# A new order for the steps of all eight chunks on TensorE, ScalarE, GpSimd and VectorE, with two waits moved into their step

## The reference

```python
# part A: projection, causal convolution of 4 taps, then running sums
z = conv(x @ in_proj_w) + conv_b                  # values, gate, scores
p_w = exp(clip(score_scale * s_raw, -20, 20)) * time_weight
phi = x5 * theta;  poly = w[0] + w[1] * x5 - w[2] * x5**2
num_re, num_im, den = cumsum([p_w*poly*cos(phi), p_w*poly*sin(phi), p_w], axis=1)
y = (re * rs * norm @ W_re + im * rs * norm @ W_im) * silu(gate) @ out_proj_w
# part B: autocorrelation with the context
corr = irfft(rfft(Q) * conj(rfft(K)), axis=2).mean(-1)
w, idx = top_k(corr, 5);  out = sum_k softmax(w)_k * roll(V, idx_k) @ Wo
# part C: 8 experts, twice (forward and inverse branch), with a router
prod = (Q_side @ V) * cumsum(K_side @ W, axis=1)
weights = softmax(gelu(Q_side @ router_w1.T) @ router_w2.T + expert_bias)
out = einsum(prod * weights, U) / n_valid
```

## Time and profile before

| | |
|---|---|
| median of 3 runs | 940.35 us (939.72 to 940.51) |
| profiled execution, first to last instruction | 936.6 us |
| around the span, against the median | 3.75 us |
| TensorE busy | 847.8 us, 91% |
| VectorE busy | 760.2 us, 81% |
| ScalarE busy | 528.3 us, 56% |
| GpSimd busy | 106.3 us, 11% |

### The profile page before, as it was taken

One profiled execution on the slowest core, in us unless ns is written; L12 is line 12 of the kernel. 1 busy time (PEld: TensorE's weight loads), 2 busy tenths in 40 slices (PEclk: granted clock), 3 DMA queues, 4 the chain that ended last, 5 costly groups with the idle time before them and its releaser, 6 DMA issues.

```text
span 936.6 us, 11711 instructions
## 1 busy us (share of the span) xinstructions
PE 847.8 (91%) x4072; PEld 505.2 (54%) x4072; DVE 760.2 (81%) x1290; ACT 528.3 (56%) x853; POOL 106.3 (11%) x206
## 2 busy tenths in 40 slices
PE   3499848999999999999999999999999998997896
PEld 1145535564756465646565465646556565656344
DVE  6898898899999997899979898999789994473232
ACT  3674871876478554875377456765476644312311
POOL 2020011200310012001200031001210031001001
PEclk9689988999999999999999999999999999999898
DMA  9860242101611052204310071004410250000000
GB/s 298 166 133 4 67 91 45 48 1 19 128 35 45 9 111 62 68 10 77 71 40 7 1 135 45 1 1 90 114 46 0 40 119 0 1 1 23 0 1 22
DMA packets 38768, 50.96 MB, mean 54 GB/s; under 512 B 15236, under 2 KB 30903, under 8 KB 38711
## 3 DMA queue, kind: packets, MB, share of 16 engines
q0 software_dynamic: 7008, 25.21, 14.1%
q1 hardware_dynamic: 31558, 24.62, 9.2%
q10 hardware_dynamic: 144, 0.39, 0.1%
HBM read 20.81 MB, written 4.19 MB: 27 GB/s over the span
## 4 chain that ended last, share of the span: by engine, by line
PE 72%; DVE 15%; ACT 7%; issue 3%; POOL 1%; DMA 0%; ACTq 0%; DVEq 0%; POOLq 0%
PE ps L791 12%; PE ps L771 11%; PE ps L780 11%; PE ps L654 6%; PE ps L593 6%; PE ps L736 4%; PE ps L576 3%; PE ps L624 3%; DVE zc L2484 3%; DVE sc L2563 3%; PE ps L453 2%; PE ps L713 2%; PE ps L638 2%; PE ps L703 2%; PE ps L788 1%
## 5 line engine op out<-in xcount | busy, mean ns | idle before, releaser
L2563 DVE TENSOR_TENSOR_SCAN sc<-mask,sc 128x1024 f32<-128x1024 bf16 x64 | 146.2, 2285 | 0.4
L780 PE MATMUL ps<-x2t,mv 128*128 128x512 f32 x256 | 123.5, 605 | 0.1
L771 PE MATMUL ps<-cum,mw 128*128 128x512 f32 x256 | 123.0, 603 | 0.0
L791 PE MATMUL ps<-up,prod 128*128 128x256 f32 x512 | 115.6, 381 | 0.1
L791 PEld LDWEIGHTS ps<-up,prod 128*128 128x128 f32 x512 | 94.8, 190 | 19.3 <-issue 5.1
L2311 POOL DMA_DIRECT2D acc<-sq x48 | 42.0, 874 | 536.0 <-ACT sq L1535 523.9
L1629 ACT ACTIVATE cs<-ps 128x512 f32<-128x512 f32 x64 | 38.0, 593 | 113.8 <-PE ps L771 113.8
L2555 DVE TENSOR_TENSOR sc<-sc,g 128x1024 f32<-128x1024 f32 x64 | 77.3, 1207 | 7.2 <-ACT sc L1519 7.2
L771 PEld LDWEIGHTS ps<-cum,mw 128*128 128x128 f32 x256 | 48.2, 192 | 62.1 <-issue 60.0
L593 PE MATMUL ps<-sc,wy 64*64 64x512 f32 x512 | 66.6, 644 | 15.2 <-DVE zc L2484 8.2
L1535 ACT ACTIVATE sq<-sc 128x1024 f32<-128x1024 f32 x48 | 50.5, 1053 | 46.3 <-DVE sc L2563 33.7
(11 more groups left out here) (248 smaller groups left out, 1446.7 us busy)
## 6 DMA issues: line engine op xcount, KB each, us to landing
acc<-sq POOLq DMA_DIRECT2D x48, 512.0 KB, 4.6
xt<-in_x_t_dram SPq DMA_DIRECT2D x8, 512.0 KB, 4.4
xs_a<-in_x_dram SPq DMA_DIRECT2D x8, 512.0 KB, 3.8
cin<-in_ctx_dram SPq DMA_DIRECT2D x8, 512.0 KB, 4.8
out_dram<-prod SPq DMA_DIRECT2D x16, 256.0 KB, 2.1
win<-in_in_proj_dram SPq DMA_DIRECT2D x1, 544.0 KB, 6.1
prod<-in_L_ffn_V_fwd_dram SPq DMA_DIRECT2D x2, 256.0 KB
prod<-in_L_ffn_W_fwd_dram SPq DMA_DIRECT2D x2, 256.0 KB
```

The costliest lines, as they stand in the source:

```text
L771: last = mm(o, mw[:, t, br, c:c + P], cum[:, t, :], start=(t == 0), stop=(t == 1))
L780: last = mm(o, mv[:, t, br, c:c + P], x2t[:, t, :], start=(t == 0), stop=(t == 1))
L791: return mm(o[:, (q % 2) * D:(q % 2 + 1) * D], prod[:, j, q * P:(q + 1) * P], up[:, j, :], start=start, stop=False)
L2563: V.tensor_tensor_scan(flat, mask[:, 0:2 * T], flat, 0.0, ALU.mult, ALU.add)\
```

## The change

No instruction is added or taken away. In the four lists the same calls stand in another order: of the 569 places of TensorE 377 hold another call, of ScalarE's 587 480, of VectorE's 577 387, of GpSimd's 81 8 (four pairs of neighbouring additions swapped). SyncE's list of transfers is as it was. Two waits that stood in TensorE's list between `fold(25)` and `b_transform(0, "cf", 0)` are now at the top of that step. Places of the lists that the steps below speak of, from TensorE, ScalarE and VectorE in turn; most of the rest is of the same kind:

```diff
@@ -630,6 +630,9 @@
             def b_transform(i, name, t):
 
                 src = ch if name == "cf" else xh
+                if is_first(i) and name == "cf" and t == 0:
+                    pe.wait_ge(folded, len(FOLD))
+                    pe.wait_ge(ready, 2)
                 pe.wait_ge(*VEC_B.at(i, "fold", 1 if name == "cf" else 3))
                 o = free_b(i, name, t)
                 for b in range(SEQ):
@@ -815,11 +818,11 @@
...
             a_scores(0)
             a_project(0, 0)
             a_project(0, 1)
-            a_spread(0, 0)
-            fold(0)
-            a_spread(0, 1)
             a_project(0, 2)
             a_project(0, 3)
+            fold(0)
+            a_spread(0, 0)
+            a_spread(0, 1)
             a_sums(0, 0)
             a_sums(0, 1)
...
             fold(8)
+            a_sums(0, 2)
+            a_sums(0, 3)
             fold(9)
             fold(10)
-            a_sums(0, 2)
-            a_sums(0, 3)
+            fold(11)
             a_squares(0)
-            fold(11)
             fold(12)
+            fold(13)
+            fold(14)
             a_factor(0, 0)
-            fold(13)
             a_factor(0, 1)
             a_scores(1)
             a_out(0, 0)
             a_project(1, 0)
             a_out(0, 1)
-            fold(14)
+            fold(15)
...
             b_back(6)
             c_out(5, 0)
             c_out(5, 1)
-            a_sums(7, 2)
             b_out(6, 0)
             b_out(6, 1)
+            a_squares(7)
+            a_sums(7, 2)
             a_sums(7, 3)
-            a_squares(7)
+            a_factor(7, 0)
             b_transform(7, "cf", 0)
+            a_factor(7, 1)
             b_transform(7, "cf", 1)
-            a_factor(7, 0)
             c_transpose(6, 0)
             c_transpose(6, 1)
-            a_factor(7, 1)
+            a_out(7, 0)
             c_hidden(6, 0)
-            a_out(7, 0)
             c_hidden(6, 1)
             a_out(7, 1)
             c_hidden(6, 2)
+            c_running(6, 0)
             c_hidden(6, 3)
-            c_logits(6)
-            c_running(6, 0)
-            c_turn(6)
...
             c_hidden(7, 3)
+            c_running(7, 0)
             c_logits(7)
-            c_running(7, 0)
+            c_running(7, 1)
             c_turn(7)
             c_own(7, 0)
+            c_own(7, 1)
             c_weights(7)
+            c_running(7, 2)
             c_spread(7, 0)
-            c_running(7, 1)
             c_spread(7, 1)
-            c_last(7, 0)
-            c_own(7, 1)
-            c_running(7, 2)
+            c_running(7, 3)
             c_spread(7, 2)
             c_own(7, 2)
-            c_running(7, 3)
             c_spread(7, 3)
+            c_spread(7, 4)
+            c_running(7, 4)
+            c_running(7, 5)
             c_own(7, 3)
-            c_running(7, 4)
-            c_spread(7, 4)
             c_own(7, 4)
-            c_running(7, 5)
+            c_own(7, 5)
             c_spread(7, 5)
-            c_own(7, 5)
             c_running(7, 6)
+            c_running(7, 7)
             c_spread(7, 6)
+            c_spread(7, 7)
+            c_last(7, 0)
+            c_last(7, 1)
             c_own(7, 6)
-            c_running(7, 7)
-            c_spread(7, 7)
-            c_last(7, 1)
+            c_own(7, 7)
             c_last(7, 2)
             c_last(7, 3)
             c_last(7, 4)
             c_last(7, 5)
-            c_own(7, 7)
...
             a_scores(0)
-            a_exp(0)
             a_project(0, 0)
             a_project(0, 1)
             a_turns(0, 0)
-            a_turns(0, 1)
+            a_project(0, 2)
+            a_project(0, 3)
+            a_exp(0)
             a_linear(0, 0)
             a_linear(0, 1)
+            fold(0)
+            a_turns(0, 1)
             a_angles(0, 0)
+            a_angles(0, 1)
             a_turns(0, 2)
-            fold(0)
-            a_angles(0, 1)
             a_turns(0, 3)
-            a_project(0, 2)
-            a_project(0, 3)
-            a_gate(0, 0)
-            a_gate(0, 1)
+            a_angles(0, 2)
+            a_angles(0, 3)
             a_guard(0)
-            a_angles(0, 2)
...
             fold(1)
+            a_gate(0, 0)
             fold(2)
...
             a_conv(0, 0)
+            a_conv(0, 1)
+            a_conv(0, 2)
+            a_fraction(0, 0)
             a_split(0)
+            a_conv(0, 3)
+            a_poly(0, 0)
+            a_fraction(0, 1)
+            a_poly(0, 1)
             a_den(0)
-            a_conv(0, 1)
-            a_fraction(0, 0)
-            a_fraction(0, 1)
-            a_poly(0, 0)
-            a_poly(0, 1)
             a_moments(0, 0)
             a_fraction(0, 2)
-            a_scan(0, 0)
             a_moments(0, 1)
             a_fraction(0, 3)
+            a_scan(0, 0)
             a_scan(0, 1)
-            a_conv(0, 2)
-            a_conv(0, 3)
             a_moments(0, 2)
+            a_moments(0, 3)
...
+            a_moments(7, 7)
             a_scan(7, 6)
-            a_moments(7, 7)
+            a_scan(7, 7)
             b_back(6)
-            a_scan(7, 7)
             c_residual(5, 0)
             c_residual(5, 1)
+            b_fold(7, "cf")
             b_residual(6, 0)
+            a_weight(7)
             b_residual(6, 1)
-            a_weight(7)
-            b_fold(7, "cf")
             a_factor(7)
```

More of the change, by code:

```diff
@@ L846, in _ @@
             a_out(0, 1)
-            fold(14)
+            fold(15)
             a_project(1, 1)
-            fold(15)
             fold(16)
             fold(17)
+            a_spread(1, 0)
+            a_project(1, 2)
             fold(18)
@@ L965, in _ @@
             a_project(3, 1)
-            a_spread(3, 0)
+            a_project(3, 2)
             c_hidden(1, 1)
@@ L1245, in _ @@
-            a_project(7, 2)
-            a_project(7, 3)
-            c_weights(5)
             b_spectrum(6, "qa")
             b_spectrum(6, "qb")
+            c_turn(5)
+            c_own(5, 0)
+            c_running(5, 1)
             b_spectrum(6, "ka")
-            c_spread(5, 0)
             b_spectrum(6, "kb")
             b_spectrum(6, "va")
+            c_weights(5)
             b_spectrum(6, "vb")
-            c_running(5, 1)
+            c_spread(5, 0)
+            c_running(5, 2)
             c_spread(5, 1)
@@ L1271, in _ @@
+            c_own(5, 5)
             b_wt(6)
-            c_own(5, 5)
-            c_running(5, 6)
             c_spread(5, 6)
+            b_wf(6)
             c_own(5, 6)
-            b_wf(6)
-            a_sums(7, 1)
             c_running(5, 7)
@@ L1280, in _ @@
             c_own(5, 7)
+            a_sums(7, 1)
             b_back(6)
@@ L1703, in _ @@
             fold(10)
+            a_gate(0, 1)
+            fold(11)
             a_norm(0)
+            fold(12)
+            fold(13)
+            fold(14)
             a_scores(1)
@@ L1775, in _ @@
             a_project(2, 0)
+            a_exp(2)
+            c_hidden(0, 0)
+            a_linear(2, 0)
+            a_turns(2, 0)
             b_transform(1, "cf", 0)
             b_transform(1, "cf", 1)
-            a_project(2, 1)
-            c_hidden(0, 0)
+            c_hidden(0, 1)
             a_layer(1)
-            c_hidden(0, 1)
             c_hidden(0, 2)
             c_hidden(0, 3)
-            a_turns(2, 0)
+            a_project(2, 1)
+            a_angles(2, 0)
+            c_logits(0)
@@ L1796, in _ @@
-            a_project(2, 2)
-            b_spectrum(1, "qa")
             b_spectrum(1, "qb")
-            b_spectrum(1, "ka")
-            a_project(2, 3)
+            c_weights(0)
+            a_angles(2, 2)
             b_spectrum(1, "kb")
-            c_weights(0)
-            c_tile(0, 0)
-            a_gate(2, 0)
-            a_gate(2, 1)
-            a_guard(2)
+            a_squares(2, 0)
+            b_spectrum(1, "va")
             c_tile(0, 1)
-            a_angles(2, 2)
-            b_spectrum(1, "va")
@@ L2145, in _ @@
+            b_spectrum(6, "qb")
+            a_turns(7, 2)
+            c_tile(5, 0)
             a_turns(7, 3)
             b_spectrum(6, "qa")
[L2147 to L2154 removed]
+            a_angles(7, 2)
+            c_exp(5)
+            b_spectrum(6, "ka")
+            a_squares(7, 0)
+            c_tile(5, 1)
@@ L2178, in _ @@
             a_turns(7, 7)
             a_squares(7, 3)
+            c_tile(5, 7)
+            a_guard(7)
+            a_angles(7, 6)
+            a_angles(7, 7)
+            a_squares(7, 4)
             b_back(6)
-            a_angles(7, 6)
-            a_squares(7, 4)
-            a_angles(7, 7)
             a_squares(7, 5)
```

1187 lines of the change are left out of this document (586 added, 601 removed).

## The result

| | before | after |
|---|---|---|
| median of the runs | 940.04 us (4 runs) | 914.33 us (913.5 to 917.62, 4 runs) |
| ratio, 95% interval | | 0.9736 (0.9717 to 0.9756) |
| span of the profiled execution | 936.6 us | 911.7 us |
| TensorE busy | 847.8 us | 833.7 us |
| mean granted clock of TensorE | 0.958 | 0.969 |

A forecast was written before the change was run, and what follows sets the result against it. TensorE was taken to bound the middle and the back, VectorE the front. 936.6 - 5.5 (front) - 3.0 (chunk 7's entry) - 4.4 (last phase) + 1 (middle) = 924.7, with 3.75 around the span 928.4 us; 8-in-10 range 920 to 939.

The forecast's parts named there:

- The two moved waits: Ahead of b_transform(0, "cf", 0): the same instruction waits at the same place of the same queue, 0 us.
- The sum: Profiled span 936.6 us less the gains, plus 3.75 us around the span, gives 928.4 us.
- The front: Chunks 0 and 1: VectorE's three waits go, less new ones; TensorE inherits the lead whole, 5.5 us won (1.6 to 7.2).
- Chunk 7 enters: Chunk 7's entry: waits and slow matmuls go, against waits for the last addition; 3.0 us won (0 to 5.85).
- The last phase: Chunk 7's end: 2.95 us of filled waits and 1.49 us of clock fall go, 4.4 us won (2.95 to 4.4).
- The middle: Between the ends: 3 us won by filled waits, 4 lost by thinner covers; 1 us lost (8 lost to 5 won).
- Rival A: Additions late at a_squares in chunks 4 to 7: four boundaries times 4 us, 16 us lost, 943.5 us; 12%.
- Rival C: ScalarE's three more table loads lie on the path: 3.8 us, 932.3 us (8.0 and 936.4 by the skill); 7%.

The follow-up runs named there:

- run of the end alone: Kernel before, with the new order only from chunk 7's entry to the end, old order up to chunk 6's scans: 931.26 us, ratio 0.9909.
- front run: Kernel before, with the new order only up to chunk 0's b_back and the old one behind it: 934.98 us, ratio 0.9946.
- kernel with half rows: Changed kernel with fold(10) to fold(14) moved later and GpSimd's six additions of chunk 0 transferring half of each row: 912.83 us, ratio 0.9710.

## Why the prediction was wrong

- **The two moved waits**: 0 forecast; TensorE waits 0.57 us at that step, against 0.56 before.
- **The sum**: the 3.75 us around the span are 1.8 in nearly all runs; by the other 1.9 the profiled execution lies under the median. The forecast goes by the median and is not moved by it.
- **The front**: 5.5 forecast, 5.5 measured alone (3.7 to 6.5). The size was right by luck, since the path was wrong: VectorE won 5.2 us up to its last scan of chunk 0 where 3.75 were forecast (its first wait is 0.85 and not gone), and all of it was lost at a_squares(0), which starts at 71.01 against 70.69. I had named the exponential as what is late next and not asked what the squares wait for. The lead came in chunk 1, where the 2.94 us wait is gone and the folds end earlier: the transforms of chunk 0's context start at 100.88 against 105.51. The wait for `cor` grew from 5.99 to 7.12 us. TensorE did not inherit it whole either: in the full new order 3.3 us are lost again at c_logits(0), a bound that I had not worked out.
- **Chunk 7 enters**: 3.0 forecast, 4.5 by the markers. The 2.32 us wait is gone, the squares wait 0.78 (forecast 1.1; 1.84 in the run of the end alone), the transposes 0.96 (forecast 1). Within the bounds.
- **The last phase**: 4.4 forecast, 5.0 measured alone, 5.7 by the markers, of which 0.8 lie in the hidden layer (8.60 us against 9.39), where nothing was changed. There is no wait behind the hidden layer any more, and the forecast is within the interval of the run (3.5 to 5.7 us).
- **The middle**: 1 lost forecast, 12.5 won measured. This is the step that failed, in three of its terms. I took 3 us for filled waits, the two longest; the smaller ones, 8.7 us together, I put at nothing, and the waits as a whole shrank by 6.3 us, from 12.1 to 5.8. I priced the 1.57 us wait at its length although at both ends of the kernel I had charged the fall behind a wait, 1.49 us, from rows; in the middle I read the mean clock, 0.99, and concluded that nothing stood there. The bound "5 won is what is left of 12.4 us if half goes" counted idle time only and left the slow busy time out. The falls behind three waits cost 4.8 us. The 4 us for thinner covers were too dear: the waits for the norm ahead of the transposes are 0.39, 0.32 and 0.96 us. The new order also puts both residuals of a chunk side by side on VectorE, which may be why; that was not tried by itself.
- **Rival A**, the late additions: 0.78 and 1.08 us at two boundaries, not 4 at each, and no fall behind either. **Rival C**: the queue has the 50 loads that I counted; what the three cost on TensorE's path was not tried. The drain that the Trainium skill adds in "ScalarE: Activation LUTs", section "What ACT_TABLE_LOAD costs", shows here as little as before:

```profile
L1397 ACT ACT_TABLE_LOAD x50 | 64.2, 1283 | 2.0 <-PEq L3496 1.2
```

What stays open: of the 13.3 us that the markers give from c_out(0) to c_out(5), 6.3 are waits (12.1 before and 5.8 after, by the table of waits from 187 us to c_out(5)) and 4.8 the three falls (1.6+1.7+1.5); what the last 2.2 us are was not tried. Why a fall comes behind one wait and not behind another stays open too. The new order of one engine was not tried with the others in the old one.

## What to carry to other kernels

On an engine that is 98% busy, count all the waits, the small ones too, and look at the matmuls behind each: where a fall follows, a wait of 1 us costs 2 to 3, and the mean clock over a long stretch hides it. Where a wait can't be filled with useful steps, useless ones of its length can give the fall back, but measure one of them first. When a lead is forecast, follow it to the next step that waits for several things, and name the slowest of them.

## What the runs showed of the hardware

- Falls of TensorE's clock (a granted clock of 0.62 to 0.73 over stretches of 4.5 to 6.3 us) come behind waits as short as 0.97 us, but not every time, and the length of the wait doesn't decide it. Behind the 1.57 us wait in chunk 4 the kernel before has one; the front run has the same wait and none:

```profile
459.01 0.50 PE L557 MATMUL ps<-pair,spreads 128*128 128x256 f32 x2 [1.58 <-DVE zc L2589]
459.73 1.06 PE L551 MATMUL ps<-xt,win 128*32 128x256 f32 x8 [0.22 <-DVE zc L2593]
460.71 1.98 PE L576 MATMUL ps<-xt,win 128*128 128x512 f32 x4
```

The 1.8 to 2.1 us of wait ahead of chunk 1's first spread have no fall in any of the eight traces of kernels that keep the old order there. The 2.5 us at c_logits(0) have one in four traces and none in two, of which this is one (the kernel with half rows):

```profile
176.59 1.06 PE L749 MATMUL ps<-prod,w2t 128*32 128x512 f32 x8 [2.54 <-ACT prod L1598]
177.58 2.05 PE L641 MATMUL ps<-fdft,xs_a 128*128 128x128 f32 x16
```

So a single profile can be off by 1 to 2 us at any such place, and what a wait costs with its falls is a mean over runs.
- A GpSimd addition of 128x4 took 2.09 us beside a scan of VectorE with two inputs in SBUF, and 0.20 in the kernel before, where the scan came later.
- In chunk 0, over four traces, an accumulating transfer of 512 KB landed 4.5 to 5.8 us after its issue when the one before was 2.4 us or more ahead, and 6.5 to 8.6 when it was about 1 to 2.1 us ahead; one of 256 KB took 3.8 to 4.8.
